# Splitting the wide softmax exponential of an attention loop into two instructions

## What is computed

```
h = layernorm(x) * (1 + ca) + sa
q = einsum('bnhd,hed->bnhe', xh, Wq)
scores = einsum('bnhe,bmhe->bhnm', q, q) / NORM
attn = softmax(scores, axis=-1)
x = x + ga * (einsum('bhnm,bmhe->bnhe', attn, q) @ Wp.T + bp)
h = layernorm(x) * (1 + cb) + sb
x = x + gb * ffn(h)
```

## Time and profile before

| what | value |
|---|---|
| median of three runs | 1964.57 us (1964.0 to 4664.26) |
| the profiled execution's own time | 1966.44 us |
| its span in the trace | 1964.6 us |
| PE, ACT, DVE, POOL busy, share of the span | 95%, 96%, 76%, 64% |
| PE clock granted, mean of the execution | 0.997 |
| the loop's wide exps | 683, from 67.0 to 1910.4 us |

### The profile page before, as it was taken

The page is one execution under the profiler, slowest core; times in us unless marked ns, Lnnn a source line. Parts: engine busy times, 40 slices in busy tenths (PEclk is TensorE's granted clock), DMA queues, the critical chain, the costliest instruction groups (busy, mean ns, idle before and its releaser), DMA issues.

```text
span 1964.6 us, 47515 instructions
## 1 busy us (share of the span) xinstructions
PE 1869.5 (95%) x18423; PEld 544.1 (28%) x18423; DVE 1486.8 (76%) x2514; ACT 1883.0 (96%) x1491; POOL 1253.8 (64%) x2104
## 2 busy tenths in 40 slices
PE   8788889999999999999999999999999999999999
PEld 6311112222222222222232222222223222322225
DVE  5567677778778877777777787778778777777873
ACT  6899999999999999999999999999999999999992
POOL 5173776478746776376773787467763767737770
PEclk9899999999999999999999999999999999999999
DMA  6531112121211211112111112111111112111100
GB/s 212 165 91 48 48 34 53 43 64 44 55 48 38 61 46 53 54 43 56 46 50 52 54 51 51 42 50 54 47 55 49 53 43 59 44 42 49 33 7 18
DMA packets 121391, 108.40 MB, mean 55 GB/s; under 512 B 21952, under 2 KB 120128, under 8 KB 120912
## 3 DMA queue, kind: packets, MB, share of 16 engines
q1 hardware_dynamic: 120416, 103.69, 18.6%
q10 hardware_dynamic: 752, 1.67, 0.2%
HBM read 96.49 MB, written 8.65 MB: 54 GB/s over the span
## 4 chain that ended last, share of the span: by engine, by line
ACT 48%; PE 29%; issue 11%; DVE 5%; POOL 4%; DVEq 0%; POOLq 0%
ACT attend_probs L890 27%; ACT attend_probs L896 20%; PE attend_sums L943 14%; PE attend_scores L929 8%; PE attend_out L951 3%; PE attend_scores L951 1%; DVE attend_probs L1148 1%; PE attend_sums L957 1%; ACT hidden L884 1%; PE attend_out L957 1%; POOL attend_spare L856 1%; DVE attend_spare L1160 1%; POOL attend_probs L863 1%; POOL attend_spare L861 1%; POOL attend_spare L858 1%
## 5 line engine op out<-in xcount | busy, mean ns | idle before, releaser
L890 ACT ACTIVATE attend_probs<-attend_scores 128x2048 f32<-128x2048 f32 x683 | 1289.7, 1888 | 12.7 <-PE attend_scores L929 11.9
L943 PE MATMUL attend_sums<-attend_probs,values 128*17 128x512 f32 x8192 | 1007.0, 596 | 10.4 <-POOL attend_probs L863 9.7
L1148 DVE COPY attend_probs<-attend_scores 128x896 f32<-128x896 f32 x574 | 625.8, 1090 | 293.1 <-PE attend_scores L929 284.6
L896 ACT ACTIVATE attend_probs<-attend_probs 128x896 f32<-128x896 f32 (+1 forms) x682 | 667.3, 978 | 4.3 <-DVE attend_probs L1148 2.7
L929 PE MATMUL attend_scores<-asks,keys 64*128 64x512 f16 x4096 | 564.2, 380 | 71.9 <-ACT attend_probs L890 65.3
L854 POOL TENSOR_TENSOR attend_spare<-attend_spare 128x256 f32<-128x256 f32 x287 | 176.3, 614 | 384.4 <-DVE attend_spare L1162 383.5
L929 PEld LDWEIGHTS attend_scores<-asks,keys 64*128 64x128 f16 x4096 | 150.4, 94 | 669.5 <-ACT attend_probs L890 538.4
L943 PEld LDWEIGHTS attend_sums<-attend_probs,values 128*17 128x17 f32 x8192 | 174.8, 96 | 517.5 <-issue 487.7
L858 POOL TENSOR_TENSOR attend_spare<-attend_spare 128x256 f32<-128x256 f32 x287 | 223.5, 779 | 23.9
L863 POOL TENSOR_TENSOR attend_probs<-attend_spare 128x256 f32<-128x256 f32 x287 | 220.4, 768 | 22.5
L861 POOL TENSOR_TENSOR attend_spare<-attend_spare,attend_probs 128x256 f32<-128x256 f32 x287 | 211.5, 737 | 23.9
(11 more groups left out here) (163 smaller groups left out, 834.3 us busy)
## 6 DMA issues: line engine op xcount, KB each, us to landing
keys<-parts_dram SPq DMA_DIRECT2D x768, 64.0 KB
keys<-parts_dram SPq DMA_DIRECT2D x256, 56.0 KB
asks<-parts_dram SPq DMA_DIRECT2D x192, 64.0 KB
start_x_in<-L_attn_x SPq DMA_DIRECT2D x8, 512.0 KB, 9.6
parts_dram<-start_q_parts SPq DMA_DIRECT2D x16, 256.0 KB, 2.5
attend_x_now<-L_attn_x SPq DMA_DIRECT2D x8, 512.0 KB, 4.2
out<-base SPq DMA_DIRECT2D x15, 256.0 KB, 2.6
asks<-parts_dram SPq DMA_DIRECT2D x64, 56.0 KB
```

The lines of the kernel that those rows point to most:

```text
L890: act.activation(place(n, 2), ps_scores[:, 0:4, :], ACT.Exp, scale=scale).then_inc(exps_done, 1)
L896: act.activation(cols, cols, ACT.Exp, scale=scale).then_inc(exps_done, 1)
L943: last = pe.matmul(ps_sums[32 * hq:32 * hq + E1, :], values[:, j + STEPS * b, (gg % Q_GROUPS) * Q_HEADS + hq, :], place(gg * PAIRS + Q_HEA ...
L1148: dve.tensor_copy(flat(n, 0, DIRECT), bank[:, 0:DIRECT]).then_inc(copied, 1)
```

## The change

The wide exp at L890 becomes a loop of two exps, one for each pair, each over two banks (128 x 1024). Each has its own wait for the scores of its pair, its own wait for a free place in `probs`, and adds one to `exps_done`. A round has three counts in place of two, and `exps_with` follows: pair i of round `at` is done at `S_RING * at + 1 + i`. Nothing else is edited; the lines behind the new loop move down by one.

```
 def exps_with(n):
     at, i = divmod(n, S_RING)
-    return 2 * at + 1 + i // 2
+    return S_RING * at + 1 + i
...
                 for at in range(ROUNDS):
                     n = S_RING * at
-                    act.wait_ge(scores_ready, n + 2)
-                    place_free(act, n + 1)
-                    act.activation(place(n, 2), ps_scores[:, 0:4, :], ACT.Exp, scale=scale).then_inc(exps_done, 1)
+                    for i in range(2):
+                        act.wait_ge(scores_ready, n + i + 1)
+                        place_free(act, n + i)
+                        act.activation(place(n + i), ps_scores[:, 2 * i:2 * i + 2, :], ACT.Exp, scale=scale).then_inc(exps_done, 1)
                     if at - BEHIND in TANH_IN:
```

## The result

The changed kernel takes 1988.18 us (median of four runs, 1987.42 to 1990.09) against 1964.87. The ratio on record, which leaves out one run of the kernel before at 4664.26 us, is 1.0116, 95% interval 1.0104 to 1.0128. It is slower by 23 us, some ten times the interval's half width of 2.4 us; the 39 us that the prediction took for the least that can be told was too coarse. The forecast was 1989. The profiled execution took 1988.34 us with a span of 1986.5, so the trace shows 21.9 us more than that of before.

A forecast was written before the change was run, and what follows sets the result against it. The prediction took ACT to bound the kernel, with the circle exp, scores, exp just under it. Price +37.6 us less 13 regained gave +24.6, so 1964.6 + 24.6 = 1989 us, range 1972 to 2012.

The forecast's parts named there:

- the circle: Attention loop: wide exp, PE's scores, next wide exp take 2.58 us, 0.02 under ACT's own round of 2.60.
- Part 1, the price: Wide exp: one more ACT instruction a round costs 0.055 us, 683 times, 37.6 us, all on the path.
- the two PSUM rows: Two profile-based estimates of an exp's fixed part when reading PSUM: 0.04 us (27 us in all) and 0.073 (50 us).
- the added waits: Waits in ACT's queue ahead of the second exp: cost nothing, their scores being complete before the first half began.
- Part 2, the regain: Scores following pair by pair win back 13 us of 29 where ACT is late, between 5 and 29.
- late rounds: Attention loop: what ACT loses to late inputs, put at 29 us, 17.0 of it named idle time.
- the undisturbed steps: ACT's start-to-start steps in the loop without delays: 1.76, 0.84, 0.95 and 0.52 us, adding up to 1816 us.
- The SBUF price: Rival, chance 0.12: each added wide exp costs SBUF's fixed 0.09 us, +48 us in all, 2013 us.
- Nothing is regained: Rival, chance 0.10: PE arrives late anyhow at the long delays, VectorE's copy holds the narrow exp; +37.6, 2002 us.
- The circle sets the pace: Rival, chance 0.08: exp, scores, exp bounds the loop, not ACT; loosening it gives -16 us, 1949 us.
- the step of 0.91: Sign of being right: the two wide exps of a round lie 0.91 us apart from start to start.
- Rows of 1.03 us: Sign of being right: two wide exp rows of about 1.03 us in each round.

The follow-up runs named there:

- the split narrow exp: Kernel before, wide exp whole, narrow exp made as two instructions (448 columns and the rest) with one count: 2011.98 us, ratio 1.0230.
- a lighter ACT: Kernel before with 128 columns fewer in each narrow exp, their exponential left out: 1947.39 us, ratio 0.9904.
- the split with coarse waits: Kernel before with the wide exp split in two, both exps waiting for all scores and PE for both exps: 1997.28 us, ratio 1.0154.
- the four exps: Changed kernel with each of its two wide exps made as two of one bank (512 columns), waits and counts unchanged: 2067.82 us, ratio 1.0515 to before.
- that pair of kernels: Kernel before and changed kernel, each with 128 columns left out of every narrow exp: 1947.39 us and 1939.33 us, ratios 0.9904 and 0.9862.
- one follower: Two runs of the kernel before with the wide exp split: only ACT follows pair by pair, 1993.02 us, or only PE does, 1990.50 us.
- lightened changed kernel: Changed kernel with 128 columns fewer in each narrow exp, their exponential left out: 1939.33 us, ratio 0.9862 to the kernel before.

## Why the prediction was right

- **ACT is the bound, the circle lies just under it.** That ACT is the bound is shown: the split narrow exp, which leaves the wide exp, the scores and PE's work as they were, adds its whole 0.09 us to the round. The circle exists, and bare it measures the 2.58 us that the prediction had put together from 1.88, 0.05 and 0.65. But what stops a lighter ACT after 0.01 of 0.107 us in the median round (2.61 to 2.60) is PE's own round. The prediction gave PE 2.49 us and a wait of 0.11 for the wide exp; the gap that it read as a wait is there too where the exp has long ended, and the wait is 0.013 us. No term of the sum was worked out from it.
- **Part 1, the price.** Right in kind, a little small: 0.055 us was forecast and 0.06 measured, 41 us instead of 37.6. The step that was off is the choice of the middle between the two PSUM rows; steps from start to start also give 0.055 after the change (1.81 to 1.82 against 1.76), because the rows' starts creep ahead of their ends. So the prediction's rule to count from start to start holds only while the overlap of the rows stays the same; where it grows, rounds from end to end are the ones that add up. That the added waits cost nothing is shown by the split with coarse waits and by the four exps: 0.06 each way.
- **Part 2, the regain.** 13 us was forecast and 18.7 came, of 24.9 us of late rounds rather than 29: the undisturbed steps, read to 0.01 us, are some 0.007 a round short, 5 us in all. About 10 of these need no following at all: they go because ACT's round is 0.06 longer while PE's work is the same. For this the prediction had only 0.055 us in each late round. PE's own 2.60 fits with more than that (argued from the rounds, not tested by itself): against 2.607 it makes up 0.01 us a round after a delay, against 2.667 it makes up 0.07, round after round. The narrow exp's waits, counted at nothing, fell too, from 4.3 to 2.1 us. The two errors, 3.4 us of price and 5.7 of regain, have opposite signs. That the time came out within a microsecond of the forecast is luck in part: the sum was better than its terms.
- **The rivals.** The SBUF price exists, 0.09 us, but for the narrow exp, not for this one. It speaks for the rule of the Trainium skill (Perfetto Trace Analysis, Optimizing Scalar/DVE Operations), about 93 ns on SBUF and 51 ns on PSUM: the runs have 0.09 and 0.06. "Nothing is regained" is wrong by the late rounds, 24.9 to 6.2. "The circle sets the pace" is wrong for the kernel before, by the same whole 0.09; what lies 0.01 us under ACT is PE's own round, which the prediction had 0.11 lower and so had no rival for. Where ACT is lightened below it the change pays, as that pair of kernels shows.
- **What was to be seen.** The round of 2.65 to 2.67, the step of 0.91 (0.905), the 4.0 us of idle time (some 5 were forecast) and pair 0's early scores came about as written. Rows of 1.03 us did not: they have a mean of 1.319.

## What to carry to other kernels

Before splitting an instruction so that others may follow its halves, look whose idle time the following could fill: here the split engine was the bound, with 25 us of late rounds to win and 41 us of instructions to pay. Price an added instruction from the steps between rows that read the same memory, and multiply. A second engine or a dependency circle that lies just under the bound is invisible in the bound engine's idle times. Before a gap of the second engine is called a wait, look at the same gap in a round where what it would wait for came early: if the gap is still there, it is the engine's own.

## What was not expected

ACT's rows became long. In order of time, ACT of the changed kernel:

```profile
239.42 1.50 ACT L897 ACTIVATE attend_probs<-attend_probs 128x896 f32<-128x896 f32 x1
240.28 2.47 ACT L891 ACTIVATE attend_probs<-attend_scores 128x1024 f32<-128x1024 f32 x2
242.11 1.48 ACT L897 ACTIVATE attend_probs<-attend_probs 128x896 f32<-128x896 f32 x1
242.95 2.47 ACT L891 ACTIVATE attend_probs<-attend_scores 128x1024 f32<-128x1024 f32 x2
```

A narrow exp lasts 1.50 us here and 1.01 at 607.38, with the same 2.67 us a round. Over many rounds without a delay the rows' starts creep ahead by some 0.02 us a round (2.649 from start to start in the median, 2.667 from end to end), so that a row begins up to 0.75 us before the one ahead of it has ended. A late input resets it: at each of the 38 places where a narrow exp's row is shorter by over 0.04 us than the one of the same width before it, an exp starts 0.022 us after the count that released it, 25 times DVE's, 13 times PE's. The mean row of the wide exp follows the order in which these kernels have late inputs: 1.048 us (split only), 1.170 and 1.197 (one follower), 1.319 (both). The lightened changed kernel, with 29.3 us of late rounds and 1.119, falls out of that order. So the length of a row seems to tell how early its inputs were there rather than what the instruction costs. No run tested what lets a row start early, and that stays open.
